# Self-attention's products with the values: from 128x128 tiles to four 64x64 tiles, placed behind the next pair's scores

## The reference

```python
q = (h @ wq).reshape(b, s, H, HD)
k = (h @ wk).reshape(b, s, H, HD)
v = (h @ wv).reshape(b, s, H, HD)
scores = jnp.einsum('bqhd,bkhd->bhqk', q, k) / np.sqrt(HD).astype(np.float32)
causal = jnp.tril(jnp.ones((s, s), bool))
scores = jnp.where(causal, scores, jnp.float32(-1000000000.0))
attn = jax.nn.softmax(scores, axis=-1)
ao = jnp.einsum('bhqk,bkhd->bqhd', attn, v).reshape(b, s, H * HD) @ wo
```

## Time and profile before

| what | us |
|---|---|
| median of 3 runs (674.62 to 675.5) | 674.62 |
| the profiled execution | 675.08 |
| its span, from the first to the last instruction | 673.3 |
| TensorE busy (98% of the span) | 662.0 |
| VectorE busy (67%) | 451.8 |
| ScalarE busy (49%) | 327.7 |
| GpSimd busy (37%) | 249.3 |

### The profile page before, as it was taken

How to read it: one execution, slowest core, us unless ns; L and a number is a source line. 1 busy time by engine, 2 the same in 40 slices (tenths; PEclk the granted TensorE clock), 3 DMA queues, 4 the chain that set the end, 5 groups by cost and what they waited for, 6 DMA issues and landing times.

```text
span 673.3 us, 14521 instructions
## 1 busy us (share of the span) xinstructions
PE 662.0 (98%) x5412; PEld 579.1 (86%) x5412; DVE 451.8 (67%) x885; ACT 327.7 (49%) x657; POOL 249.3 (37%) x337
## 2 busy tenths in 40 slices
PE   7999999999999999999999999999999999999997
PEld 5788888888888889989998989988887878888886
DVE  4777775786865777585677678746557777655555
ACT  5756656667653344343344333354465444444443
POOL 2321121121223343334333345416544455555553
PEclk9999999999999999999999999999999999999999
DMA  6513112011011212322222222103332223333332
GB/s 210 182 48 95 48 49 72 25 39 35 24 33 48 63 64 67 96 65 75 79 64 63 63 64 64 38 27 94 93 94 79 81 85 87 93 93 93 93 93 95
DMA packets 35865, 50.07 MB, mean 74 GB/s; under 512 B 4064, under 2 KB 22880, under 8 KB 35808
## 3 DMA queue, kind: packets, MB, share of 16 engines
q1 hardware_dynamic: 35376, 48.89, 24.6%
q10 hardware_dynamic: 432, 0.39, 0.2%
HBM read 48.22 MB, written 1.05 MB: 73 GB/s over the span
## 4 chain that ended last, share of the span: by engine, by line
PE 90%; DVE 4%; ACT 2%; issue 1%; DMA 1%; POOL 0%; SPq 0%; DVEq 0%; ACTq 0%
PE acc L546 22%; PE bank_k L519 15%; PE bank_q L519 15%; PE bank_v L519 7%; PE bank_v L622 7%; PE bank_s L666 5%; PE bank_s L519 4%; PE bank_p L687 2%; PE bank_p L652 2%; PE bank_p L697 2%; PE bank_t L697 2%; PE bank_t L674 2%; PE bank_q L643 2%; PE bank_k L632 1%; ACT pv_hi L984 1%
## 5 line engine op out<-in xcount | busy, mean ns | idle before, releaser
L546 PE MATMUL acc<-wo_hi,pv_hi 128*128 128x256 f32 x328 | 94.3, 287 | 0.2 <-DVE pv_lo L1332 0.2
L546 PE MATMUL acc<-wo_lo,pv_hi 128*128 128x256 f32 x328 | 92.7, 283 | 0.0
L546 PE MATMUL acc<-wo_hi,pv_lo 128*128 128x256 f32 x328 | 92.1, 281 | 0.0
L1468 POOL TENSOR_TENSOR wq_lo<-raw_a,wq_hi 128x256 fp32r<-128x256 f32 x32 | 24.1, 753 | 144.3 <-DVE wq_hi L1269 144.3
L1468 POOL TENSOR_TENSOR wq_lo<-raw_m,wq_hi 128x256 fp32r<-128x256 f32 x50 | 41.7, 834 | 72.4 <-DVE wq_hi L1288 68.2
L905 ACT ACTIVATE kt<-bank_k 128x512 f32<-128x512 f32 x64 | 38.4, 600 | 60.8 <-PE bank_k L519 60.8
L546 PEld LDWEIGHTS acc<-wo_hi,pv_hi 128*128 128x128 f32 x328 | 61.5, 188 | 3.4 <-issue 0.4
L1332 DVE TENSOR_TENSOR pv_lo<-rows_t,pv_hi 128x512 fp32r<-128x512 f32 (+1 forms) x51 | 39.0, 766 | 38.0 <-ACT pv_hi L984 38.0
L546 PEld LDWEIGHTS acc<-wo_lo,pv_hi 128*128 128x128 f32 x328 | 61.8, 188 | 1.9
L546 PEld LDWEIGHTS acc<-wo_hi,pv_lo 128*128 128x128 f32 x328 | 62.0, 189 | 0.0
L519 PE MATMUL bank_q<-xt_hi,wq_hi 128*128 128x512 f32 x146 | 59.7, 409 | 1.6 <-POOL wq_lo L1468 1.0
(11 more groups left out here) (196 smaller groups left out, 1902.7 us busy)
## 6 DMA issues: line engine op xcount, KB each, us to landing
raw_m<-in_chunk_m SPq DMA_DIRECT2D x50, 256.0 KB, 2.7
raw_a<-in_head_a SPq DMA_DIRECT2D x48, 192.0 KB, 2.6
raw_b<-in_head_b SPq DMA_DIRECT2D x32, 256.0 KB, 3.0
raw_m<-in_chunk_m SPq DMA_DIRECT2D x50, 128.0 KB, 2.1
raw_v<-in_pair_v SPq DMA_DIRECT2D x16, 256.0 KB, 2.8
raw_b<-in_head_b SPq DMA_DIRECT2D x32, 128.0 KB, 2.1
xs<-in_x SPq DMA_DIRECT2D x6, 128.0 KB, 3.2
out<-xs SPq DMA_DIRECT2D x3, 256.0 KB, 2.4
```

The costliest lines, as they stand in the source:

```text
L546: last = nc.tensor.matmul(acc[t // 2][:, (t % 2) * D:(t % 2 + 1) * D], w[:, tok], m, start=begins and n == 0, stop=True, skip_group_check= ...
L1468: nc.gpsimd.tensor_tensor(lo, raw, hi, ALU.subtract).then_inc(signal, 1)
```

## The change

Seven edits belong together.

1. head_values now takes the turned weights as they come out of the transposes (rows_t, 64 keys of one sequence on each half of the partitions) and multiplies 64 keys by 64 of the head's 128 columns by 64 queries: for each of 8 groups (head, tile), 2 column halves c and 2 sequences r, 32 products a pair. Sequence r stands on rows 64r to 64r+63 and writes to value_bank(r); column half c writes to partitions 64c to 64c+63. Four consecutive products thus use four different quarters of the array, and both heads are in both banks.
2. On TensorE's queue head_values(prev) stands directly behind scores(u), one pair later than before, and output(prev) behind the projections of queries and keys of head 0 of nxt. In the last pair, where nxt is an expert chunk, there are no such projections, and output(prev) comes directly behind head_values(prev). The very last pair of stage b (not deferred) keeps its products at its own end, as well as having those of the pair before.
3. output waits for both halves of pv_lo at once, as each bank holds both heads.
4. ScalarE and VectorE make pv_hi and pv_lo of prev between their steps of u: ScalarE before the exponentials, VectorE behind subtract_max.
5. take_turned is one copy of 128 partitions into rows_t, and one signal.
6. vs has two buffers by the pair's parity, as pair u's values are written while prev's are still wanted; take_v waits for pv_done of two pairs back.
7. hh moves from rows_t to a new place in the tile of the cross-attention's raw weights; attn_t and its memset are gone.

```diff
-        self.deferred = kind == "a" and not (self.last and half == HALVES - 1)
+        self.deferred = not (self.last and half == HALVES - 1)
...
-        vs = sb("vs", [P, NT, PAIR])
+        vs = [sb(f"vs{p}", [P, NT, PAIR]) for p in range(2)]
...
-        attn_t = sb("attn_t", [P, G, SPB, SEQ])
...
-        hh = rows_t[:].rearrange("p n h q -> p (n h q)")
+        hh = raw_a[:, 0:HT]
...
@@ -383,6 +383,10 @@
         def query_bank(u, h):
             return bank_v if u.kind == "a" and h else bank_q
 
+        def by_sequence(ap, row):
+
+            return ap.rearrange("p h (n r q) -> p h n r q", r=SPB, q=SEQ)[:, :, :, row, :]
+
         def value_bank(h):
             return (bank_p, bank_t)[h]
 
@@ -557,7 +561,7 @@
                         pe.wait_ge(A["vo_lo"], u.n)
                     add_output(u, h, vo_hi[:, 2 * u.i + h, :], vo_lo[:, 2 * u.i + h, :]).then_inc(A["wo_done"], 1)
                 else:
-                    pe.wait_ge(B["pv_lo"], u.of(h))
+                    pe.wait_ge(B["pv_lo"], u.of(1))
                     pe.wait_ge(B["wo_lo"], u.of(h))
                     add_output(u, h, wo_hi[h][:], wo_lo[h][:]).then_inc(B["wo_done"], 1)
 
@@ -688,14 +692,21 @@
                                                 rows_t[rows, n], start=True, stop=True)
                 last.then_inc(A["pv_done"], 1)
 
-            def head_values(u, h):
+            def head_values(u):
 
                 pe.wait_ge(B["vs"], 2 * u.n)
-                pe.wait_ge(B["attn_t_lo"], u.n)
                 pe.wait_ge(B["attn_t"], u.n)
-                for n in range(NT):
-                    last = nc.tensor.matmul(value_bank(h)[:, n * P:(n + 1) * P], vs[:, n, h * P:(h + 1) * P],
-                                            attn_t[:, h * NT + n, :, :], start=True, stop=True)
+                turned = rows_t[:].rearrange("p n h q -> p (n h q)")
+                values = vs[u.n % 2]
+                for g in range(G):
+                    h, n = divmod(g, NT)
+                    cols = slice(g * SEQ, (g + 1) * SEQ)
+                    for c in range(P // SEQ):
+                        width = slice(h * P + c * SEQ, h * P + (c + 1) * SEQ)
+                        for r in range(SPB):
+                            rows = slice(r * SEQ, (r + 1) * SEQ)
+                            last = nc.tensor.matmul(value_bank(r)[c * SEQ:(c + 1) * SEQ, cols], values[rows, n, width],
+                                                    turned[rows, cols], start=True, stop=True)
                 last.then_inc(B["pv_done"], 1)
 
             def turn_tokens(step, banks):
@@ -782,27 +793,27 @@
 
                 prev, nxt = u.prev(), u.next()
                 scores(u)
-                for h in range(2):
-                    output(prev, h)
-                held = prepare(u)
+                if prev.kind == "b":
+                    head_values(prev)
                 if nxt.kind == "b":
                     project_queries(nxt, 0)
                     project_keys(nxt, 0)
-                else:
+                for h in range(2):
+                    output(prev, h)
+                if nxt.kind == "m":
                     project_gate(nxt)
+                held = prepare(u)
                 turn_attn(u)
                 if nxt.kind == "b":
                     project_queries(nxt, 1)
                     project_values(nxt, False)
+                    project_keys(nxt, 1)
+                    project_values(nxt, True)
                 else:
                     project_up(nxt)
-                release(held[:1])
-                for h in range(2):
-                    head_values(u, h)
-                if nxt.kind == "b":
-                    project_keys(nxt, 1)
-                    project_values(nxt, True)
-                release(held[1:])
+                release(held)
+                if not u.deferred:
+                    head_values(u)
 
             def chunk(u):
                 prev, nxt = u.prev(), u.next()
...
 
                 act_e.wait_ge(B["v_done"], 2 * u.n - (not second_tiles))
-                if u.n > 1:
-                    act_e.wait_ge(B["pv_done"], u.of(1) - 2)
+                if u.n > 2:
+                    act_e.wait_ge(B["pv_done"], u.n - 2)
                 at = second_tiles * (NT // 2)
-                nc.scalar.activation(vs[:, at:at + NT // 2, :], bank_v[:].rearrange("p (t n) -> p t n", n=PAIR),
+                nc.scalar.activation(vs[u.n % 2][:, at:at + NT // 2, :], bank_v[:].rearrange("p (t n) -> p t n", n=PAIR),
                                      ACT.Copy).then_inc(B["vs"], 1)
 
             def log_q(u):
@@ -948,9 +959,7 @@
 
             def take_turned(u):
                 act_e.wait_ge(B["t_done"], u.n)
-                for r, signal in ((0, B["attn_t_lo"]), (1, B["attn_t"])):
-                    rows = slice(r * SEQ, (r + 1) * SEQ)
-                    nc.scalar.activation(attn_t[rows, :, r, :], groups(bank_t[rows, :]), ACT.Copy).then_inc(signal, 1)
+                nc.scalar.activation(rows_t[:].rearrange("p n h q -> p (n h q)"), bank_t[:], ACT.Copy).then_inc(B["attn_t"], 1)
 
             def take_context_values(u):
 
@@ -959,9 +968,10 @@
                     nc.scalar.activation(by_row(pv_hi[:], r), value_bank(r)[:].rearrange("p (h b n) -> p h b n", h=2, n=P),
                                          ACT.Copy).then_inc(A["pv_hi"], 1)
 
-            def take_head_values(u, h):
-                act_e.wait_ge(B["pv_done"], u.of(h))
-                nc.scalar.activation(pv_hi[:, h], value_bank(h)[:], ACT.Copy).then_inc(B["pv_hi"], 1)
+            def take_head_values(u):
+                act_e.wait_ge(B["pv_done"], u.n)
+                for r in range(SPB):
+                    nc.scalar.activation(by_sequence(pv_hi[:], r), by_tile(value_bank(r)[:]), ACT.Copy).then_inc(B["pv_hi"], 1)
 
             def take_value_out(u):
                 act_e.wait_ge(A["vo_done"], u.n)
@@ -1019,27 +1029,25 @@
                 nxt = u.next()
                 after = nxt.next()
                 take_v(u, True)
+                if u.prev().kind == "b":
+                    take_head_values(u.prev())
                 exponentials(u)
-                late = piece_at(u)[0] == "logits"
-                if not late:
-                    prepare(u)
                 if nxt.kind == "b":
                     take_k(nxt, 0)
                     if after.kind == "m":
                         split_up(after, nxt.of(0))
+                prepare(u)
                 take_turned(u)
-                if late:
-                    prepare(u)
                 if nxt.kind == "m":
                     gate(nxt)
                 prepare(u, 1)
-                for h in range(2):
-                    take_head_values(u, h)
                 if nxt.kind == "b":
                     take_v(nxt, False)
                     take_k(nxt, 1)
                     if after.kind == "m":
                         split_up(after.next(), nxt.of(1))
+                if not u.deferred:
+                    take_head_values(u)
 
             def split_down(u):
 
@@ -1212,9 +1220,11 @@
                     nc.vector.tensor_tensor(by_row(pv_lo[:], r), value_bank(r)[:].rearrange("p (h b n) -> p h b n", h=2, n=P),
                                             by_row(pv_hi[:], r), ALU.subtract).then_inc(A["pv_lo"], 1)
 
-            def split_head_values(u, h):
-                v.wait_ge(B["pv_hi"], u.of(h))
-                nc.vector.tensor_tensor(pv_lo[:, h], value_bank(h)[:], pv_hi[:, h], ALU.subtract).then_inc(B["pv_lo"], 1)
+            def split_head_values(u):
+                for r in range(SPB):
+                    v.wait_ge(B["pv_hi"], u.of(r))
+                    nc.vector.tensor_tensor(by_sequence(pv_lo[:], r), by_tile(value_bank(r)[:]), by_sequence(pv_hi[:], r),
+                                            ALU.subtract).then_inc(B["pv_lo"], 1)
 
             def scale_scores(u):
 
@@ -1387,6 +1397,8 @@
                 after = nxt.next()
                 scale_scores(u)
                 subtract_max(u)
+                if prev.kind == "b":
+                    split_head_values(prev)
                 if nxt.kind == "b":
                     split_values(nxt)
                 normalise(u)
@@ -1406,8 +1418,8 @@
                     prepare_piece(*piece_at(u), u)
                 if nxt.kind == "b":
                     take_q(nxt, 1)
-                for h in range(2):
-                    split_head_values(u, h)
+                if not u.deferred:
+                    split_head_values(u)
                 if nxt.kind == "m":
                     weigh_gate(nxt)
                     multiply_up(nxt)
```

More of the change, by code:

```diff
@@ L199, in flamingo_layer @@
     E = 16
-    SETUP = 6
+    SETUP = 5
     TOP = 6
@@ L257, in flamingo_layer @@
         gqk = sb("gqk", [P, 1])
-        raw_a1 = [sb(f"raw_a1_{p}", [P, A1]) for p in range(2)]
+        raw_a = sb("raw_a", [P, 2 * A1])
+        raw_a1 = [raw_a[:, p * A1:(p + 1) * A1] for p in range(2)]
```

(5 more changed lines are left out.)

## The result

| | before | after |
|---|---|---|
| median of the runs, us | 674.75 (4 runs) | 665.35 (4 runs) |
| profiled execution, us | 675.08 | 664.52 |
| its span, us | 673.3 | 662.6 |

The ratio, of the means, is 0.986, with a 95% interval of 0.984 to 0.987: 9.6 us less (9.4 between the medians), where 7.1 less were forecast. The direction is as forecast, and so are the parts of the mechanism that the sum named; a wait of TensorE that the change removed as well was not in the sum.

What follows compares the result with a forecast made beforehand. TensorE was taken to bound the kernel, busy 662.0 of 673.3 us; -9.2 (14 full pairs), -1.8 (first) and +3.8 (last) gave -7.2 us: 667.9 profiled, 667.5 median, range 665.5 to 670, up to 676 with C and D.

Steps and rivals of the forecast that it cites:

- the sum: Whole kernel: 14 full pairs -9.2 us, first pair -1.8, last pair +3.8, together -7.2 us.
- Four tiles to a slot: Values' products on TensorE: four records share a 0.056 us slot, so 64 records take 16 slots, 0.90 us a pair.
- A: Values' products: two tiles share a slot, not four; 2.02 us with shape changes, median 681 us; chance 15%.
- B: Values' products: no overlap or tiles blocking each other; 3.58 + 0.23 us a pair, some 709 us; chance 4%.
- D: Values' products: partial overlap, three to a slot or 0.08 us slots; -0.36 us a pair, median 672; chance 7%.
- Changes of tile shape: Around the values' products on TensorE: 0.33 us added less 0.10 already paid, net 0.23 us a pair.
- The path to pv_lo: ScalarE copies and VectorE subtractions: pv_lo ready at T + 4.6, 0.4 us before TensorE needs it, no wait.
- rival C: Full pairs: pv_lo comes later than counted, say by 0.7 us; +0.3 in 14 pairs, median 672; chance 6%.
- The last pair: End of the self-attention stages: TensorE stands 2.4 us, then 1 us more; 15.4 against 11.56 us, +3.8.
- the one on vs: ScalarE's queue: second vs buffer gains nothing by itself, as the vs copy stood directly behind pv_hi's; lets products be late.
- the price of the old pair: Old values' products on TensorE, per pair: 1.70 for the records plus 0.09 for the next projection, 1.79 us.
- The forecast's 0.66: Each full pair: products fall from 1.79 to 1.13 us, so the pair is 0.66 us shorter.

Runs made afterwards that it cites:

- The two orders of two tiles: Changed kernel with its 32 products reordered so neighbours differ only in columns, or only in rows: 677.40 us (ratio 1.005) and 676.38 us (1.002).
- the kernel before with the copy first: Kernel before, with ScalarE's copy of the next pair's first values to vs moved ahead of the two pv_hi copies: 674.24 us, ratio 0.999.
- the changed kernel again: The changed kernel run again without edits, as a base for the runs beside it: 666.02 us, ratio 0.986 against the kernel before.
- the memset back: Changed kernel with a memset of the same size, on unit_w, where that of attn_t stood at the start: 665.24 us, ratio 0.986.
- the tiles alone: Kernel before with the 64x64 products, but the old place, one vs and the old order on every queue: 672.30 us, ratio 0.996.
- the place alone: Changed kernel's order and two buffers of vs, but the old 128x128 products on attn_t: 676.24 us, ratio 1.002 against the kernel before.
- the stand filled: Changed kernel, last pair: next stage's gate and up projections ahead of the output products, second head's output behind the turn: 662.05 and 662.19 us, ratio 0.981.

## Why the prediction was right, and where it fell short

**Four tiles to a slot: right.** 16 slots of 0.058 us, forecast 0.056. Rivals A, B and D fall by the 1.09 us of the 64 records. The two orders of two tiles show what A would have been: 1.84 us of products and 676.4 to 677.4 us in all, where the prediction priced A at 681: it had 2.02 us a pair for these products with their changes of shape, where about 1.85 came, and it left out the wait that the change removes.

**Changes of tile shape: right but for small sizes.** Read in pair 6: the products with their way in and out take 1.09 us, forecast 1.12 (0.90 and 0.22); the projection behind them is 0.11 to 0.12 longer (1.49 for 1.38 and 1.37), forecast 0.11; the output behind a projection is 0.10 shorter, as forecast. Behind the old products the projection lost 0.14 (1.51 for 1.37), where I had 0.09; 0.03 of that is the wait below, since the kernel before with the copy first has 1.48. Both halves of the values' projection became 0.03 shorter as well (1.42 to 1.39, and 1.51 without the wait to 1.48), for which the sum has no term; why is open. Together that is the 0.11 us a pair by which these sizes were short.

**The path to pv_lo: right.** No wait for it in pairs 1 to 14, rival C falls, and T + 4.5 in the last.

**The last pair: right,** +3.9 for +3.8, in the executions where the clock holds. What was not foreseen is that its stand of 2.4 us lets the clock fall in some executions (7 of the 12 runs in the result, of the changed kernel again, and with the memset back), at 1.4 us each (234.3 against 232.9 to the last record). That is most of why the runs gained 9.6 and not the 10.6 between the two profiled executions: two of the four had the fall, and the profiled one had not.

**The step that failed** is the one on vs: "The second buffer of vs gains nothing by itself: the copy to vs stood directly behind that of pv_hi in ScalarE's queue". The buffer itself indeed gains nothing: the kernel before with the copy first has one buffer and gains the 0.15. What failed is that the copy's place behind pv_hi was taken to cost nothing before the change, so the price of the old pair, 1.79 us for its products, left out a wait of TensorE for that copy. These rows of TensorE, just behind the earlier trace rows, show it:

```profile
317.14 0.39 PE L519 MATMUL bank_k<-xt_hi,wk_lo 128*128 128x512 f32 x1
317.40 0.36 PE L622 MATMUL bank_v<-wv_hi,xt_hi 128*128 128x256 f32 x1
317.60 0.28 PE L622 MATMUL bank_v<-wv_lo,xt_hi 128*128 128x256 f32 x1
```

In rows 8 the copy starts at 316.67 and takes 0.59, so bank_v is free at 317.26, and the second half of the values was due at 317.37, 0.23 behind the keys' last product at 317.14. That is 0.11 us of room, and the product starts 0.14 behind the copy's end. I looked at what the copy waits for and not at who waits for the copy. The values' projection started at 317.40, 0.03 late, and its second product at 317.60, 0.20 behind it and not 0.12: 0.11 us a pair in these rows. The list of waits does not name it. The other 0.04 of the 0.15 is in the next pair's projections of queries and keys (1.40 us each against 1.38), and why is open. Moving the products away takes both copies of pv_hi from in front of this one. Priced by the runs, per pair:

| step | pair, us | difference |
|---|---|---|
| before | 14.90 | |
| copy to vs first | 14.75 | -0.15: the wait |
| and tiles of 64x64 (with two buffers of vs) | 14.24 | -0.51: products -0.61, way into them +0.09 |
| and products behind the scores | 13.98 | -0.26: fewer changes from one kind of product to another |

The forecast's 0.66 is the sum of the last two, 0.77, less the 0.11 of small sizes above; the wait's 0.15 was missing. Over the 14 full pairs the two make 3.4 us (12.65 against 9.2) of the 3.5 between -7.2 and -10.7. With the wait alone in the sum, 15 times 0.15, the forecast would have been about 665.3 us. That this meets the measured time so closely is luck: the small sizes gain 1.5 us more, and the falls of the clock (0.9 us in the mean of the four runs) take over half of that back. The same rows also held the trap: with the tiles alone the copy comes due earlier against its queue, and 0.49 of 0.66 us a pair are given back (14.73 against 14.24 with the copy first).

That the last 0.26 is changes of kind is read from the distances in the two traces and not from a run of its own: the output is 0.10 shorter (2.98 to 2.88), the first half of the values 0.12, the second keys 0.12 and the second half of the values 0.03, and the first queries are 0.11 longer. It belongs to the new tiles: with the old products the place beyond the wait is worth 0.08 us (14.75 with the copy first, 14.67 with the place alone).

## What to carry to other kernels

When a product on the busy engine gets shorter, look at each copy that frees a PSUM bank behind it: measure from its end to the start of the product that needs the bank, and if that is near zero, the saving turns into a wait unless the copy goes ahead of less urgent ones. An earlier copy, with the buffer beside it, was worth 6.6 us here on top of the new tiles, about as much as the new place of the products (7.0, from 672.30 to 665.35). Price the ends of a pipelined stage on their own and give the drain some independent work: filling a stand of 2.4 us gained 2.5 us, and more where the clock had fallen.

## What was not expected of the hardware

- Four tiles of 64x64 start within 0.02 us and share a slot of 0.058 us, as long as the slot that two tiles share (0.0575), be they neighbours in rows or in columns; 64 fp32 records take 1.09 us, 17 ns each.
- A stand of TensorE of 2.4 us left its clock at the higher level in some executions and let it fall to 1.2 GHz for most of the next 4 us (0.59 on average) in others of the same kernel. With the stand filled it fell in none of ten.
- Behind a short wait a projection of the values pays twice: its first product starts late by the wait (0.03 us before, 0.35 with the tiles alone), and its second comes after 0.20 in place of 0.12 us in both.
